# Slot attentions with a ring of score banks: the maximum is turned before the output and the late projection piece

## The reference, cut to what matters

```python
def _L2_attn_b_ref(x, Wq, bq, Wk, bk):
    q = (x @ Wq + bq).reshape(B, N, H, Dh).transpose(0, 2, 1, 3)
    k = (x @ Wk + bk).reshape(B, N, H, Dh).transpose(0, 2, 1, 3)
    v = k
    scale = C ** (-0.5)
    attn = jnp.einsum('bhnd,bhmd->bhnm', q, k) * scale
    attn = jax.nn.softmax(attn, axis=-1)
    out = jnp.einsum('bhnm,bhmd->bhnd', attn, v)

def _encoder_layer(x, ...):
    ...
    o = jnp.einsum('bhqk,bhkd->bhqd', attn, v).transpose(0, 2, 1, 3).reshape(b, s, d)
    o = o @ ow.T + ob
    x = _layernorm(x + o, n1w, n1b)
    ff = jax.nn.relu(x @ l1w.T + l1b) @ l2w.T + l2b
    return _layernorm(x + ff, n2w, n2b)
```

## Time and profile before

| | us |
|---|---|
| median of three runs (3564.74 to 3572.22) | 3570.16 |
| the profiled execution | 3577.13 |
| its span | 3575.1 |

### The profile page before, as it was taken

One profiled execution on the slowest core, in us unless ns is written; L12 is line 12 of the kernel. 1 busy time (PEld: TensorE's weight loads), 2 busy tenths in 40 slices (PEclk: granted clock), 3 DMA queues, 4 the chain that ended last, 5 costly groups with the idle time before them and its releaser, 6 DMA issues. The chain is left out here.

```text
span 3575.1 us, 61234 instructions
## 1 busy us (share of the span) xinstructions
PE 2842.3 (80%) x23920; PEld 1873.6 (52%) x23920; DVE 2019.2 (56%) x4357; ACT 1382.7 (39%) x2886; POOL 961.6 (27%) x1321
## 2 busy tenths in 40 slices
PE   4689699887899688876866999867778687677776
PEld 1233477655577555554445666544445455344444
DVE  5998655466645757434643666645555455455553
ACT  4344144343344233223432554434444334344442
POOL 1455332133322200031032333301111245011112
PEclk7789799898899778777977999989999799799997
DMA  1000100010000000020000000021111010211111
GB/s 72 0 1 0 48 1 1 8 28 13 1 1 2 1 1 1 4 76 19 22 17 16 1 1 1 1 66 45 59 59 59 23 28 19 66 45 58 58 57 37
DMA packets 46939, 90.95 MB, mean 25 GB/s; under 512 B 6052, under 2 KB 34524, under 8 KB 45888
## 3 DMA queue, kind: packets, MB, share of 16 engines
q1 hardware_dynamic: 44608, 86.43, 7.8%
q0 software_dynamic: 2048, 0.61, 0.1%
HBM read 70.16 MB, written 19.14 MB: 25 GB/s over the span
## 5 line engine op out<-in xcount | busy, mean ns | idle before, releaser
L750 ACT ACTIVATE s_sT<-s_R 128x1024 f32<-128x1024 f32 (+2 forms) x448 | 400.0, 945 | 201.6 <-PE s_R L684 200.8
L785 DVE TENSOR_REDUCE s_negm<-s_R 128x4 f32<-128x1024 f32 x320 | 376.9, 1220 | 94.9 <-PE s_R L655 86.6
L655 PE MATMUL s_R<-s_qk 32*128 32x256 f32 (+2 forms) x3584 | 260.3, 407 | 63.0 <-ACT s_sT L750 35.9
L757 ACT ACTIVATE s_oc<-s_OB 128x256 f32<-128x256 f32 x224 | 86.0, 384 | 546.6 <-PE s_OB L703 546.6
L715 PE MATMUL s_X<-all_ident,s_negm 128*128 128x128 f32 x448 | 95.2, 295 | 231.3 <-ACT s_oT L1179 54.1
L684 PE MATMUL s_R<-s_qA,s_qk 32*128 32x256 f32 (+2 forms) x3584 | 243.0, 385 | 16.1 <-DVE s_negm L785 10.7
L800 DVE TENSOR_TENSOR s_qA<-s_qk,s_X 128x256 f32<-128x256 f32 x224 | 93.4, 417 | 286.7 <-PE s_X L715 286.7
L703 PE MATMUL s_OB<-s_sT,s_v 128*32 128x256 f32 (+2 forms) x3584 | 246.7, 397 | 9.7 <-ACT s_sT L750 6.4
L655 PEld LDWEIGHTS s_R<-s_qk 32*128 32x128 f32 x3584 | 163.0, 196 | 109.0 <-issue 91.7
L684 PEld LDWEIGHTS s_R<-s_qA,s_qk 32*128 32x128 f32 x3584 | 164.2, 187 | 80.1 <-issue 66.1
L2492 POOL TENSOR_TENSOR all_hT<-s0s_hs,s0s_cb 128x1024 f32<-128x1024 f32 x64 | 150.6, 2354 | 196.9 <-DVE s0s_hs L2526 178.8
(11 more groups left out here) (571 smaller groups left out, 6325.3 us busy)
## 6 DMA issues: line engine op xcount, KB each, us to landing
s_wB<-enc_b SPq DMA_DIRECT2D x32, 962.5 KB, 4.8
s_scratch<-s_pk SPq DMA_DIRECT2D x51, 256.0 KB, 2.0
s_qk<-s_scratch SPq DMA_DIRECT2D x204, 64.0 KB
s_wA<-enc_a SPq DMA_DIRECT2D x32, 193.0 KB, 4.1
big<-moe SPq DMA_DIRECT2D x2, 2347.0 KB, 11.5
big<-routed SPq DMA_DIRECT2D x2, 2084.0 KB
all_W<-weights SPq DMA_DIRECT2D x1, 2296.0 KB, 16.4
all_W<-weights SPq DMA_DIRECT2D x1, 2295.5 KB, 11.4
```

Source lines behind the costliest of these rows:

```text
L655: last = pe.matmul(S[h][:, t * T:t * T + hi - lo], b.qk[rows, r % 2, 0, c, t * P:(t + 1) * P], b.qk[rows, r % 2, 1, c, lo:hi], start=(t == ...
L750: act.activation(b.sT[:, u % (a.lag + 1), 2 * p:2 * p + 2, 0:a.width], b.R[:, a.turned_at(u, p), 0:a.width], ACT.Exp).then_inc(s.expd, 1)
L785: ins = dve.tensor_reduce(b.negm[:, u % 2, :, at].rearrange("p t h -> p h t"), S.rearrange("p h (t k) -> p h t k", t=TT), AX_X, ALU.max, n ...
```

## The change

In both stages PE turns the maximum of step u+1 right behind the transposed scores of step u, ahead of the turned output and the late pieces; DVE adds it ahead of the division; and the numbering of X puts the turned maximum before the late pieces. ACT's and POOL's programs stay as they are. No instruction is added or taken away.

```diff
@@ SlotPlan
         for u in self.steps:
-            order += self.early(u) + self.late(u)
+            order += self.early(u)
             if u + 1 < self.U:
                 order.append(("m", u + 1))
+            order += self.late(u)
@@ slot_attention_stage and encoder_stage, PE
                     if 0 <= u < U:
                         slot_turned_scores_pe(pe, a, b, u)
+                    if u + 1 < U:
+                        slot_turn_max_pe(pe, g, a, b, u + 1)
                     if 0 <= u - a.lag < U:
                         slot_turn_out_pe(pe, g, a, b, u - a.lag)
                     for item in a.late(u):
                         other(item)
-                    if u + 1 < U:
-                        slot_turn_max_pe(pe, g, a, b, u + 1)
@@ encoder_stage, DVE (slot_attention_stage alike)
+                    if u + 1 < U:
+                        slot_add_max_dve(dve, a, b, u + 1)
                     if 0 <= u - a.lag < U:
                         slot_norm_dve(dve, a, b, u - a.lag)
-                    if u + 1 < U:
-                        slot_add_max_dve(dve, a, b, u + 1)
```

## The result

The changed kernel takes 3365.0 us (median of four runs, 3361.55 to 3369.15) against 3567.89 us (four runs, 3564.74 to 3572.22): a ratio of 0.9431, 95% interval 0.9415 to 0.9447. The forecast was 3365. The profiled execution has a span of 3364.3 us.

What follows compares the result with a forecast made beforehand. PE was taken to be bound by waiting for tile X behind ACT's copy of the late piece. From the median 3570.16 us, 165.5 us of waits and 39.5 us of clock falls gave 3365 us, range 3345 to 3385, reaching to 3410.

Steps and rivals of the forecast that it cites:

- What bounded it: Before the turned maximum, PE waited in 141 of 224 steps for ACT to copy the late piece from X: 220.7 us.
- The working of a step: Steps with a late piece: next scores start sooner, by 0.65 to 1.45 us a step; 165.5 us in all.
- The hop from DVE to PE: From the end of an engine's work to PE's start, before the late piece: taken as 0.10 us.
- What was next: Check whether exponentials, ACT's copy or the next maxima come late for PE after the change: all judged in time.
- The 83 steps without a late piece: Only the order of two pairs of transposes changes there: cost 0, or 17 us if a 0.2 us wait were uncovered.
- The clock: 25 falls of PE's clock behind long idle times in encoder and plain stages all go: 25 x 1.58 = 39.5 us.
- The sum: Whole kernel: waits and clock falls together gain 205.0 us, from the median 3570.16 to 3365.2 us.
- The signs: Trace marks of being right, such as late pieces waiting 0.2 to 0.4 us for qA and a shorter first encoder stage.
- Falls that stay: Rival: clock falls remain because PE does only transposes and a short wait before the next scores; 3405 us, chance 0.10.
- A second wait: Rival: each of the 141 steps loses half its gain to a wait before scores, value matmuls or turned maximum; 3467 us, 0.07.
- Slower, PE held for DVE: Rival: the turned maximum, ahead of everything, holds PE until DVE's late maxima and additions end; 3611 us, chance 0.03.

Runs made afterwards that it cites:

- The two kernels with filled idle time: Kernel before, with two unused matmuls (3526.83 us) or four unused transposes (3529.84 us) added ahead of each turned maximum that stands behind a late piece.
- the transposes: Kernel before, with four unused 128x128 transposes added ahead of each turned maximum behind a late piece: 3529.84 us, ratio 0.9882.
- The experiment that goes one group further: Changed kernel, with PE's turned maximum moved ahead of the transposed scores of the step instead of behind them: 3597.83 us, ratio 1.0069 to the kernel before.
- the first group of experiments: The first four experiments; the kernel before, run beside them, took 3569.69 us (median of seven runs).
- the output's place: Changed kernel, with PE turning the output first, then the maximum, then the late piece: 3378.37 us, ratio 0.9463 to the kernel before.

## Why the prediction was right, step by step

**What bounded it.** That PE waited for the tile X behind ACT's queue, and not for data, held: moving only ACT's copy took back 114 us of the 220.7.

**The working of a step.** It had 1.38 us from the turned maximum to the next scores in a step with two transposes as late piece; the trace has 1.32. The hop from DVE to PE was taken as 0.10 between 0.05 and 0.15; it is 0.05 (the addition ends at 2450.60, PE starts at 2450.65). The `y` piece puts the turned maximum 0.18 us later than in the other steps, where 0.14 was taken. Kind by kind, from the transposed scores to the next scores (median, us), a step gained 1.41 with `t1` (forecast 1.37), 1.50 with `t` (1.45), 1.14 with `v` (1.13), 1.00 with `f2` (1.01), 1.39 with the plain `h` (1.28), 0.95 in the causal stage (0.87) and 0.77 in the window stage (0.65). Added up over all steps that is 168 us where 165.5 was forecast. Four encoder steps were put at 23.90 us and take 23.79.

**What was next.** No second wait took the place. Before the scores PE waits 33.5 us for the exponential, 74 times, in the steps without a late piece, and before the value matmuls 6.4 us; in the kernel before it was 35.9 and 6.4. The 83 steps without a late piece cost nothing, as assumed.

**The clock.** All 25 falls went, and two more, which the sum had left out: the second fall of each encoder stage followed the same kind of wait. The two kernels with filled idle time, which lost the same 27, put the price at 40 to 43 us in the order of before, against 39.5 in the sum.

**The sum.** The stages gained 212.9 us where 205.0 were forecast: some 3 us more from the waits and up to 4 from the clock. The profiled executions differ by 211.1 us (3577.13 and 3366.05), the medians by 202.9: the profiled execution of the kernel before was 9 us above its median, that of the changed kernel 1 us. So the forecast of 3365 met the median to the microsecond by luck. The mechanism and each term were right within a few us, and 8 us too little in the sum met 8 us of scatter between executions.

**The signs.** The first encoder stage lost 92 us, a little more than the 85 to 90 that the forecast's 395 to 400 us stood for. The late pieces wait 0.29 us for `qA`, within 0.2 to 0.4.

**The rivals.** Falls that stay: out, by the trace and by the transposes. A second wait: out. Slower, PE held for DVE: it did not happen. The experiment that goes one group further shows that the mechanism is real and that the sign turns there, though 80 us of its waits before the turned maximum (47.6 + 26.0 + 6.7, ACT's copies of `qk`, `f1` and `v`) came from early pieces that the rival did not name.

## What to carry to other kernels

When several users share one tile in a fixed order, look at which engine frees it and where that release stands in its queue: a user on the critical path should not stand behind one whose reader is busy with something long. Move it forward only until the next thing it needs is just ready; one group further it waits for its data and for the users ahead of it. And price an idle time of PE together with the clock that follows it: here it added a quarter to what the waits themselves cost.

## What the runs showed that was not expected

**The part between the causal and the plain stage moves by itself.** No kernel here changes it, yet it takes 775 to 791 us from the last turned maximum of the one to the first of the other. The same stretch of the kernel before, of the changed one, and of the one with DVE's order undone:

```profile
857.78:1646.25 788.47, 639.03 (x4587) 0.82 0.03 10
```

```profile
852.20:1642.92 790.72, 638.76 (x4588) 0.82 0.03 10
```

```profile
855.25:1630.68 775.43, 625.13 (x4588) 0.84 0.03 10
```

The shortest has the higher granted clock, 0.84 against 0.82, and PE is busy 14 us less with the same matmuls; it spends 241 us at 1.2 GHz where the others spend 277. The same spread shows among the executions of one kernel: the seven of the kernel before beside the first group of experiments go from 3562.23 us at a mean granted clock of 0.893 to 3583.03 at 0.886. What decides where the clock falls there is not shown. A difference of 10 us between two of these kernels can come from this alone, so the small ones (13 us for the output's place) have to be read from the stages themselves.

**Work of no use made the kernel faster.** With two matmuls or four transposes more in 141 places it is 1.2 to 1.3% faster than without, because PE's clock stays up: 27 falls fewer.
